# A two-layer graph kernel on one core: the 32 packing products of a chunk placed one by one between the 32 products of a half chunk

## The reference

```
Wh = h @ W
e = (Wh @ a1)[:, None] + (Wh @ a2)[None, :]
e = where(e > 0, e, 0.2 * e); e = where(adj > 0, e, -9e15)
h_prime = softmax(e, axis=1) @ Wh
x = layernorm(x + elu(h_prime))            # layer 0
x1 = a @ x / sum(a, axis=1)                # a = adj as float
x = layernorm(x + concat([x1, x]) @ weight + bias)   # layer 1
```

## Time and profile before

| | us |
|---|---|
| median of three executions | 1636.6 |
| the profiled execution | 1634.6 |
| its span | 1632.8 |
| TensorE busy with matmuls | 1562.7 (96%) |
| ScalarE busy | 1003.1 (61%) |
| VectorE busy | 889.4 (54%) |
| packing products, line 682, 4096 of them | 121.2 |

### The profile page before, as it was taken

One profiled execution on the slowest core, in us unless ns is written; L12 is line 12 of the kernel. 1 busy time (PEld: TensorE's weight loads), 2 busy tenths in 40 slices (PEclk: granted clock), 3 DMA queues, 4 the chain that ended last, 5 costly groups with the idle time before them and its releaser, 6 DMA issues.

```text
span 1632.8 us, 46669 instructions
## 1 busy us (share of the span) xinstructions
PE 1562.7 (96%) x16966; PEld 1375.6 (84%) x16966; DVE 889.4 (54%) x3323; ACT 1003.1 (61%) x2513; POOL 479.3 (29%) x583
## 2 busy tenths in 40 slices
PE   7379999999999999999999999998999999999998
PEld 6268888888888888888888888887888888888887
DVE  6885555555555565555555555554445454454443
ACT  3768999899989989998999899982000010000100
POOL 0654433443443344334433443440000000000000
PEclk9589999999999999999999999999999999999999
DMA  8537787778777777777777777743000000000000
GB/s 266 194 129 272 274 283 280 271 278 280 285 272 276 280 278 270 281 271 272 273 280 284 273 276 283 284 163 86 20 16 16 16 17 19 16 16 16 19 16 16
DMA packets 100859, 302.82 MB, mean 185 GB/s; under 512 B 5856, under 2 KB 68064, under 8 KB 68064
## 3 DMA queue, kind: packets, MB, share of 16 engines
q1 hardware_dynamic: 100832, 302.48, 51.9%
HBM read 289.77 MB, written 12.68 MB: 185 GB/s over the span
## 4 chain that ended last, share of the span: by engine, by line
PE 92%; issue 1%; DVE 0%; ACT 0%; POOL 0%; DVEq 0%; POOLq 0%
PE acc L718 55%; PE acc L780 28%; PE pack_ps L682 6%; PE turn_ps L804 2%; PE turn_ps L794 1%; DVE factors L942 0%; POOL one L388 0%; ACT level_ring L619 0%; DVE stats L971 0%; DVE row_sums L1016 0%; DVE rows_y L1034 0%; ACT part_sums L613 0%; DVE rows_y L983 0%; DVE row_sums L1021 0%; DVE mv L978 0%
## 5 line engine op out<-in xcount | busy, mean ns | idle before, releaser
L508 ACT ACTIVATE level_ring<-s_row,cols 128x256 fp8e4<-128x256 f32 x2048 | 839.3, 498 | 4.9 <-DMA s_row<-s_and_t 4.9
L718 PE MATMUL acc<-factors,edge_ring 128*128 128x258 f16 x4096 | 544.5, 274 | 35.2 <-DVE factors L942 27.5
L718 PE MATMUL acc<-factors,level_ring 128*128 128x258 f16 x4096 | 543.5, 274 | 0.0
L780 PE MATMUL acc<-factors,adj_ring 128*128 128x258 f16 x4096 | 470.5, 274 | 5.0 <-issue 5.0
L718 PEld LDWEIGHTS acc<-factors,edge_ring 128*128 128x128 fp8e4 x4096 | 392.1, 98 | 94.6 <-DVE factors L942 27.8
L780 PEld LDWEIGHTS acc<-factors,adj_ring 128*128 128x128 fp8e4 x4096 | 400.4, 98 | 64.1 <-issue 5.2
L718 PEld LDWEIGHTS acc<-factors,level_ring 128*128 128x128 fp8e4 x4096 | 400.9, 98 | 60.4
L928 DVE TENSOR_TENSOR level_ring<-level_ring,edge_ring 128x1024 uint16<-128x1024 uint16 x256 | 187.8, 735 | 239.2 <-ACT level_ring L508 231.4
L935 DVE TENSOR_TENSOR edge_ring<-edge_ring,level_ring 128x1024 uint16<-128x1024 uint16 x256 | 195.9, 796 | 0.0
L611 ACT ACTIVATE part_sums<-acc 128x258 f32<-128x258 f32 x32 | 12.4, 386 | 298.1 <-PE acc L780 298.1
L386 POOL TENSOR_SCALAR one<-mv 128x2 f32<-128x2 f32 x64 | 24.7, 386 | 552.6 <-DVE mv L978 552.6
(11 more groups left out here) (102 smaller groups left out, 861.4 us busy)
## 6 DMA issues: line engine op xcount, KB each, us to landing
adj_ring<-in_adj SPq DMA_DIRECT2D x128, 2048.0 KB, 7.7
x_parts<-parts SPq DMA_DIRECT2D x32, 129.0 KB, 4.7
factors<-x_parts SPq DMA_DIRECT2D x8, 516.0 KB, 3.9
factors<-in_x SPq DMA_DIRECT2D x16, 256.0 KB, 3.3
s_row<-s_and_t SPq DMA_DIRECT2D x32, 128.0 KB, 4.6
rows_x<-in_x SPq DMA_DIRECT2D x32, 128.0 KB, 4.3
x_rows<-rows_y SPq DMA_DIRECT2D x32, 128.0 KB, 7.8
rows_x<-x_rows SPq DMA_DIRECT2D x32, 128.0 KB, 2.1
```

Source lines behind the costliest of these rows:

```text
L508: a = act.activation(level_bytes[:, h % MASK_SLOTS, j, :, :], s_halves[:, slot, :, :], ACT.Relu, bias=t_big[:, h * HALF + j:h * HALF + j + ...
L718: m = pe.matmul(acc[a][:, 0:ROW], mask, factors[:, neg, jj, :], start=(jj == 0), stop=(jj == NJ - 1))
L780: m = pe.matmul(acc[b][:, 0:ROW], ring_1_bytes[:, c, j, b, :], factors[:, 0, jj, :], start=(jj == 0), stop=(jj == NJ - 1))
```

## The change: what it does

`pack_tile(c, i)` issues a single packing product. `multiply` gets an argument `pack_chunk`: where it is given, a packing product follows each of the 32 products of the half chunk. `group` gives it for the odd half chunks, where `pack(c)` stood behind before. `mask_used` and `acc_done` stay on the same products of line 718 as before, and `packed` stays on the last packing product. The four packings of group 0's own words, ahead of the first group, stay in a row.

```
-            def multiply(g, h, factors_in=False, first=False):
+            def pack_tile(c, i):
+                j, t = i // TPG, i % TPG
+                low_bytes = adj_ring[:, c % ADJ_SLOTS, t, j * P:(j + 1) * P].bitcast(F8)\
+                    .rearrange("p (c b) -> p c b", b=4)[:, :, 0]
+                words_t = pack_ps[c % 2][:, j * WPG:(j + 1) * WPG].rearrange("p (w t) -> p w t", t=TPG)[:, :, t]
+                return pe.matmul(words_t, low_bytes, pack_w[:, :], start=True, stop=True)
...
+            def multiply(g, h, factors_in=False, first=False, pack_chunk=None):
...
                         m = pe.matmul(acc[a][:, 0:ROW], mask, factors[:, neg, jj, :],
                                       start=(jj == 0), stop=(jj == NJ - 1))
-                    if h == 7 and a < 2 * TPG - 1:
-                        m.then_inc(acc_done, 1)
-                m.then_inc(mask_used, 1)
+                        if h == 7 and a < 2 * TPG - 1 and j == HALF - 1:
+                            m.then_inc(acc_done, 1)
+                        if a == 2 * TPG - 1 and j == HALF - 1:
+                            m.then_inc(mask_used, 1)
+                        if pack_chunk is not None:
+                            w = pack_tile(pack_chunk, a * HALF + j)
+                if pack_chunk is not None:
+                    w.then_inc(packed, 1)
...
                         if h % 2 and not last:
                             packable(g + 1, c)
-                        multiply(g, h, first and h % 2 == 0, first)
-                    if not last:
-                        pack(c)
+                        multiply(g, h, first and h % 2 == 0, first, c if h % 2 and not last else None)
```

More of the change, by code:

```diff
@@ L673, in packable @@
                     pe.wait_ge(words_ok, UPG * g + c - 1)
-            def pack(c):
[L677 to L682, removed]
+            def pack_tile(c, i):
[4 more added lines that the diff above has]
+                return pe.matmul(words_t, low_bytes, pack_w[:, :], start=True, stop=True)
+            def pack(c):
+                for i in range(UNIT * TPG):
+                    m = pack_tile(c, i)
                 m.then_inc(packed, 1)
```

## The result

The changed kernel took 1616.05 us (median of four executions, 1614.73 to 1617.2), the kernel before, with one execution more, 1635.28 us (1633.3 to 1637.88). The ratio is 0.9881, 95% interval 0.9863 to 0.9899. Between the medians lie 19.2 us, and by the interval the gain is 16.5 to 22.4 us. The profiled execution took 1614.73 us, its span is 1612.9 us.

The account below looks back on a forecast made before the run. TensorE's own stream was taken to bound the kernel (92% of the span). Closing the hole at 29 turns gains 11.9 us, packing pairs 0: 1636.6 - 11.9 = 1624.7 us, own range 1620 to 1629, 8 in 10 1616 to 1638.

Parts of the forecast that it names:

- The turn of the loop: Layer 0 loop's branch: TensorE's hole of 0.41 us (turn 0.83 minus cover 0.42) closes 29 times, 11.9 us gained.
- The cover: Work handed out ahead of the loop's branch: 8.5 long products and as many packing products, 1.16 us against 0.83.
- The packing products: 3968 single packing products between long ones: taken to cost 0 ns more per pair; 3.0 ns would eat the gain.
- their ordinary price: Steps into and out of a packing row, on record: 25 ns per packing product, about 0.1117 us per long product.
- bounds of -25 and +72 ns: Per pair: packing product vanishes beside the long one (-25 ns), or its weight load shows at full 97 ns (+72).
- The masks: Masks of half chunks 2 and 3, from VectorE, stay hidden; coming late was counted with "no change" (0.12).
- the 2.0 us of room: Time between VectorE's mask and TensorE's need of it in the loop: 3.2 us before, 2.0 us after the change.
- group 31: End of layer 0, behind the loop: said to be untouched by the change, as layer 1.
- the room that those signals lost: Signals on acc3's last product: it starts 0.14 us before the next group instead of 1.32, 1.18 us less room.
- ScalarE: At line 519 its wait of 0.56 us for acc2 shrinks to -0.05 us: it gets there just in time.
- The bound of about 31.3 us for a pass: Much faster rival (0.05): packing products vanish, ScalarE's round (31.3 us) or transfers (31.2 us) then bind; 1609 us.
- a median of 1636.6 us: Starting point of the forecast for the median, 2.0 us above the profiled execution's 1634.6 us.

Follow-up runs that it names:

- last_chunk: Changed kernel, but only the last chunk's 32 packing products of a group stand one by one, the other three packings are rows: 1619.51 us, one execution.
- twos: Changed kernel, but two packing products stand behind every second product instead of one behind each: 1622.6 us, one execution.
- first_three: Changed kernel, but only the first three packings of a group stand one by one, the last, ahead of the branch, is a row: 1632.42 us, one execution.
- both: Changed kernel with rows of factors 264 places apart: 1603.52 us, ratio 0.9813 to the kernel before.
- align264: Kernel before with rows of factors 264 places (528 B) apart instead of 258, w1 and bias loaded late into level_ring: 1613.53 us, ratio 0.9879.
- align260b: Kernel before with rows of factors 260 places (520 B) apart, w1 and bias moved into level_ring: 1624.28 us, one execution.

## Why the prediction was right or wrong

**The turn of the loop: right, in mechanism and size.** 0.41 us, 29 times, 11.9 us. The kernel with the row ahead of the last 8 products has just this part: pass 31.81 us. The cover was sized right as well (1.16 us forecast, 1.19 found), and the dose with two products behind the row gave 0.24 us where the same arithmetic gives 0.23.

**The packing products: the term of the sum that was mis-sized.** The prediction took 0 ns per pair, "since both steps are on record at their ordinary price", between bounds of -25 and +72 ns. This is the step that failed. It was -1.5 ns, 3968 x 1.5 ns = 6.0 us. The ordinary price of a product, 111.7 ns, was an average over products that follow products, and in it lay 2.5 ns for rows of factors that don't begin at a multiple of 16 B. Behind a packing product they don't show in the product's step, and only 1 ns comes back in the packing step. The prediction looked at the step into a row of packing products and at the step out of it. The saving is in the step after that, from the product behind a packing product, and in the kernel before that product was always one with j = 0, whose row begins at a multiple of 16 B and which took 109.2 ns in any place. The trace of before had the sign of it: steps of 109, 113, 112, 113 ns, and dividing 3.58 us by 32 hides it.

**The masks: right in the loop, wrong behind it.** In the 30 passes of the changed kernel TensorE waits for no mask. The timeline of TensorE in group 31, which has no packing, shows the wait:

```profile
1087.74 1.05 PE L722 MATMUL acc<-factors,level_ring 128*128 128x258 f16 x8
1089.58 1.05 PE L722 MATMUL acc<-factors,edge_ring 128*128 128x258 f16 x8 [0.79 <-DVE edge_ring L942]
```

There TensorE would take 8 half chunks in 28.6 us, and the 2.0 us of room that were worked out for the loop don't last to the seventh. I had left group 31 out as untouched. It costs 0.8 us, once. In the kernel before the same product is 0.11 us late by starts, too little for the view of waits. The wait of 0.8 us is there in every kernel with rows 258 places apart whose last products of `acc3` stand behind packing products of the last chunk: the changed one, last_chunk, twos, and the rows ahead of the last 8 and of the last 2 products. The last of these still has a hole of 0.24 us. It isn't there in first_three, where 96 pairs stand one by one but the last packing is a row. So it goes with the room that those signals lost, as the prediction worked it out for the loop, and not with the pairs.

**ScalarE: right.** The forecast was that it would get to line 519 just in time. Timeline of ScalarE after, answering to the earlier trace rows:

```profile
601.47 0.42 ACT L524 ACTIVATE part_sums<-part_sums 128x256 f32<-128x256 f32 x1 [1.84 <-POOL part_sums L409]
...
623.74 0.83 ACT L519 ACTIVATE part_sums<-acc,cols 128x258 f32<-128x258 f32 x2
```

The two copies of line 519 now run back to back, without the 0.56 us of waiting, and TensorE doesn't notice.

**The bound of about 31.3 us for a pass, from ScalarE's round and the transfers:** the changed kernel, at 31.60 us, stays above it. With aligned rows ScalarE's round is met at 31.36 to 31.38 us, close to the estimate. The transfers, 284 GB/s over one such pass, did not show as a wait of TensorE; whether they bind just below that was not tried.

**What is left.** Between the two profiled executions lie 19.9 us (1634.6 to 1614.73). The loop gives 18.1 us by starts (29 x 0.61 us, and less in the last pass, which has no turn); group 31 takes 0.8 back. The other 2.6 us lie in the start and in the rest. A part is seen in the granted clock late in group 0 of before and of after (same columns as the earlier trace rows):

```profile
112.00:128.00 16.00, 16.00 (x155) 13.41 (x153) 9.97 (x35) 10.11 (x26) 5.27 (x6) 0.89 0.56 219
```

```profile
110.00:126.00 16.00, 14.73 (x176) 13.11 (x177) 10.84 (x33) 11.62 (x30) 4.83 (x6) 1.00 0.66 254
```

Before, the granted clock was 0.97 from 112 to 113 us, 0.50 in each of the next three, 0.82 from 116 to 117 and 1.00 behind that. At 0.50 a product of 258 columns took 215 ns from start to start, where it took 111.7 at 1.00. By the 0.89, some 3.5 us of these 16 ran at 0.50, which costs about 1.7 us by estimate (the steps about twice as long); after, the granted clock was 1.00 in all 16. In both kernels TensorE had waited for VectorE's factors at each even half chunk of group 0; before, the last such wait took 3.0 us, up to 111.76, and the clock fell about 1 us after it. Of all eleven profiles this late stretch at 0.50 is missing in the four where the last packing of a group stands in ones or twos (after, last_chunk, twos, both), and there in five of the seven where it is a row (missing in align264 and align260b). Seven executions of the kernel before, in the first group, have mean clocks from 0.980 (1636.51 us) to 0.985 (1632.91 us), so the clock varies that much in one and the same kernel. Whether the order of packing in group 0 makes the late stretch rarer stays open. The forecast also started from a median of 1636.6 us of three executions; the four medians of the same kernel since are 1635.28, 1634.12, 1635.08 and 1634.63 us, so 1.3 to 2.5 us of the distance from 1624.7 to 1616.05 us are the starting point. With the 6 us of the pairs and 1.7 us of the clock, less the 0.8 us of group 31, that makes 8.2 to 9.4 us of 8.65; whether the clock took the same course in the executions without a profile isn't shown.

## What to carry to other kernels

Ahead of a loop's branch put instructions that keep the engine busy for longer than the turn takes its sequencer (0.83 to 0.84 us here), and count that cover as the instructions in flight (here 17 matmuls and 16 of their weight loads) times the duration of each: the order of the same instructions was worth 0.41 us a turn. Look at the single steps between starts, and not only at their average: a pattern of long and short steps of the same instruction (here 112.5 and 109.2 ns) can be a cost of its own, and here it was the larger find (20.6 us in the kernel before for padding a row from 516 to 528 B, a multiple of 16). Where an engine wins a lead in a loop, follow the lead into the code behind the loop too.

## What the runs showed of the hardware

- A product of 128x258 fp16 took 109.2 ns behind a matmul of 8 columns whatever its row's start address (the changed kernel, and the one with both changes). Behind another product it took 112.5 ns where the row begins off a multiple of 16 B, 109.2 ns where it begins on one and the product ahead doesn't (rows 258 and 260 places apart), and 110.0 ns with all rows on such multiples (264 places).
- Matmuls of 8 columns, each with its own 128x128 fp8 weights, went at 25.0 ns in a row (the kernel before) and at 26.0 ns one by one between long products (the changed kernel). In the half chunk of the changed kernel from 596.76 to 601.08 us the loads of the masks were recorded at 96 ns each and those of the packing tiles at 97 ns, while the steps were 109.2 and 26.0 ns.
- At the loop's end TensorE's sequencer was 17 matmuls and 16 of their weight loads ahead of the array in all eleven profiles, whether these were all short (0.43 us), with two long ones (0.60 us) or with eight (1.1 to 1.2 us). In the five kernels with a hole it took 0.83 to 0.84 us from there to the next group's first product.
- At a granted clock of 0.50 a product of 128x258 fp16 took 215 ns from start to start (the kernel before, 113 to 116 us), at 1.00 it took 111.7 ns.
